# Attention pass of a graph network: seven tiles' sums ahead of the wait for the next batch, and one signal for seven tiles

## What is computed

```python
h = (x @ W_gat).reshape(n, H, C)
a_s = jnp.sum(h * att_src, axis=-1)
a_d = jnp.sum(h * att_dst, axis=-1)
e = a_s[src] + a_d[dst]
e = jnp.where(e >= 0, e, NEG_SLOPE * e)
m = jax.ops.segment_max(e, dst, num_segments=n)
alpha = jnp.exp(e - m[dst])
den = jax.ops.segment_sum(alpha, dst, num_segments=n)
alpha = alpha / den[dst]
msg = h[src] * alpha[..., None]
agg = jax.ops.segment_sum(msg, dst, num_segments=n)
```

## Time and profile before

| | us |
|---|---|
| median of 3 runs | 6590.89 |
| lowest and highest | 6564.43, 6594.76 |
| the profiled execution | 6602.38 |
| its span | 6600.6 |
| in it, from the first gather of the attention pass to its end | 2194.8 to about 3600 |

### The profile page before, as it was taken

The page is one execution under the profiler, slowest core; times in us unless marked ns, Lnnn a source line. Parts: engine busy times, 40 slices in busy tenths (PEclk is TensorE's granted clock), DMA queues, the critical chain, the costliest instruction groups (busy, mean ns, idle before and its releaser), DMA issues.

```text
span 6600.6 us, 99072 instructions
## 1 busy us (share of the span) xinstructions
PE 4910.2 (74%) x36573; PEld 4058.1 (61%) x36573; DVE 2714.1 (41%) x7772; ACT 1025.3 (16%) x2929; POOL 1522.1 (23%) x1600
## 2 busy tenths in 40 slices
PE   2888378787776244444445549999999999999998
PEld 2555255555554234434434238888888888888887
DVE  5888444454444445444446452222222222222222
ACT  3888311111112000000000320000000000000000
POOL 1000155565552455555553000000000000000000
PEclk8999688888887566666666779999999999999999
DMA  3111211111110222222221024444444444444444
GB/s 115 75 74 75 61 51 53 50 53 49 49 50 23 72 68 72 71 64 64 70 72 46 0 74 150 146 146 151 146 151 146 146 151 146 151 146 146 151 146 146
DMA packets 235594, 629.91 MB, mean 95 GB/s; under 512 B 64193, under 2 KB 129639, under 8 KB 235104
## 3 DMA queue, kind: packets, MB, share of 16 engines
q1 hardware_dynamic: 184688, 520.10, 24.0%
q0 software_dynamic: 50688, 107.11, 6.1%
HBM read 568.80 MB, written 58.59 MB: 95 GB/s over the span
## 4 chain that ended last, share of the span: by engine, by line
PE 64%; DVE 12%; issue 10%; another core or an unknown queue 10%; ACT 3%; SPq 1%; DMA 1%; POOL 0%; DVEq 0%; ACTq 0%; POOLq 0%
PE ps L1384 23%; PE pt L1384 17%; PE ps L1221 11%; PE pt L1421 4%; PE ps L1410 3%; PE ps L1272 2%; DVE E L1742 2%; ACT A L855 1%; PE pt L1205 1%; DVE B L1797 1%; DVE arena L1838 1%; ACT E L1057 1%; DVE C L1528 1%; PE ps L1353 1%
## 5 line engine op out<-in xcount | busy, mean ns | idle before, releaser
L1221 PE MATMUL ps<-E,arena 128*128 128x288 f32 (+7 forms) x3116 | 876.7, 437 | 316.2 <-DVE E L1742 238.7
L723 POOL DMA_INDIRECT arena<-table,src_i x782 | 743.1, 950 | 1209.0 <-DMA table<-A 667.6
L738 POOL DMA_INDIRECT E<-gat_table,src_i x782 | 754.1, 964 | 739.9 <-DVE arena L1838 382.5
L1221 PEld LDWEIGHTS ps<-E,arena 128*128 128x128 f32 x3116 | 551.8, 210 | 580.0 <-DVE E L1742 270.1
L1384 PE MATMUL ps<-E,arena 128*128 128x256 f16 x6860 | 762.0, 274 | 108.5 <-DVEq L1994 97.3
L1384 PEld LDWEIGHTS ps<-E,arena 128*128 128x128 fp8e4 x6860 | 674.6, 98 | 190.9 <-issue 109.7
L1384 PE MATMUL ps<-A,arena 128*128 128x256 f16 x6860 | 762.1, 274 | 14.0 <-DVE A L2017 14.0
L1384 PEld LDWEIGHTS ps<-A,arena 128*128 128x128 fp8e4 x6860 | 674.8, 98 | 96.4 <-issue 15.2
L1742 DVE SCALAR_TENSOR_TENSOR E<-arena,pt 128x512 f32<-128x512 bf16 x782 | 553.4, 744 | 318.0 <-PE ps L1221 223.1
L1272 PE MATMUL ps<-arena,B 128*128 128x144 f32 x2332 | 537.5, 384 | 60.9 <-issue 58.6
L1384 PE MATMUL pt<-E,arena 128*128 128x256 f16 x5145 | 567.4, 273 | 0.0
(11 more groups left out here) (305 smaller groups left out, 4115.8 us busy)
## 6 DMA issues: line engine op xcount, KB each, us to landing
arena<-adj SPq DMA_DIRECT2D x497, 784.0 KB, 4.3
adj<-E SPq DMA_DIRECT2D x49, 784.0 KB, 3.3
O<-dst_rows SPq DMA_DIRECT2D x112, 224.0 KB
arena<-table,src_i POOLq DMA_INDIRECT x782
E<-gat_table,src_i POOLq DMA_INDIRECT x782
E<-in_etype SPq DMA_DIRECT2D x781, 16.0 KB
weight_e<-tile_flags SPq DMA_DIRECT2D x216, 32.0 KB
rel_i<-tile_flags SPq DMA_DIRECT2D x216, 32.0 KB
```

Source lines behind the costliest of these rows:

```text
L723: pool.indirect_dma_start(out=rows_ring[:, k % RING, :], out_offset=None, in_=table, in_offset=bass.IndirectOffsetOnAxis(ap=src_i[:, k:k + ...
L738: pool.indirect_dma_start(out=att_rows[:, b % 3 * AB + at, :], out_offset=None, in_=gat_table, in_offset=bass.IndirectOffsetOnAxis(ap=src_ ...
L1221: mm = pe.matmul(ps[m % 4][:, (lo - WD * m) * BASES:(hi - WD * m) * BASES], rows_ring[:, k % RING, :], m_ring[:, k % MS, lo - first_dst(k) ...
```

## The change

In PE's round the sums of tiles 0 to 6 of batch b-1 come first, ahead of the wait for `staged` and of the turn of batch b. Then k runs from 0 to 6 alone: two expansions of batch b and the sum of tile 7 + k of batch b-1. The carrying products and the transposes stay after k = 2 and k = 5. `aggregated` is raised once for each half of seven tiles (and at the last tile), and the values that ACT and DVE wait for are counted in halves.

```diff
@@ ACT @@
-                            act.wait_ge(sem("aggregated"), near_last[i] + 1)
+                            act.wait_ge(sem("aggregated"), near_last[i] // AH + 1)
...
-                            act.wait_ge(sem("aggregated"), AB * (b - 1))
+                            act.wait_ge(sem("aggregated"), 2 * (b - 1))
@@ PE @@
-                    mm.then_inc(sem("aggregated"), 1)
+                    if k % AH == AH - 1 or tile == TILES - 1:
+                        mm.then_inc(sem("aggregated"), 1)
 
                 for b in range(ABATCHES + 1):
+                    if b >= 1:
+                        for k in range(AH):
+                            aggregate(b - 1, k)
                     if b < ABATCHES:
                         pe.wait_ge(sem("staged"), b + 1)
                         if b:
                             pe.wait_ge(sem("joined"), b)
                         pe.transpose(heads_turned, stage[:, b % 2, :, :].rearrange("p h t -> p (h t)"), ident[:, :]
                                      ).then_inc(sem("turned"), 1)
-                    for k in range(AB):
-                        if b < ABATCHES and k < AH:
+                    for k in range(AH):
+                        if b < ABATCHES:
                             expand(b, 2 * k)
                             expand(b, 2 * k + 1)
                         if b >= 1:
-                            aggregate(b - 1, k)
+                            aggregate(b - 1, AH + k)
@@ DVE @@
-                        dve.wait_ge(sem("aggregated"), min(AH * (g - 2), TILES))
+                        dve.wait_ge(sem("aggregated"), g - 2)
...
-                        dve.wait_ge(sem("aggregated"), AB * (b - 1))
+                        dve.wait_ge(sem("aggregated"), 2 * (b - 1))
```

## The result

The changed kernel takes 6625.25 us (median of 20 runs, 6586.99 to 6658.07), the kernel before, run beside it, 6584.44 us (20 runs, 6541.41 to 6620.12). The ratio is 1.0069, with a 95% interval of 1.005 to 1.0089: **slower by 0.7%**, some 41 us. The forecast was +89 us. The direction and most of the picture in the trace were right; the size was about twice what came.

What follows compares the result with a forecast made beforehand. It took PE's signals, late while POOL gathers, as the bound; 74 us over 49 batches plus 15 us at the end made +89 us, 6691 us profiled, 6680 us as median; range 6380 to 6850 us.

Steps and rivals of the forecast that it cites:

- The bound: Attention pass: no engine full; PE's signals reach waiters late while POOL gathers, stopping POOL about 7.5 us a batch.
- step 3: PE: seven sums of 6.5 us put the turn 6.3 us after POOL's restart R, the scan 4.7 us later.
- The edge at R+8: PE's signals: prompt until about 8 us after POOL's restart R, late behind that.
- Step 4: Carry, transposes and last expansions move into the late stretch: 26.5 us a batch for 24.98, together +89 us.
- the pattern's 25.3: Batch from 2305.78: POOL's gathers 17.5 us, late signal 2.4, DVE and ACT until restart 5.3.
- rival C: No change: every batch exactly like the one from 2305.78, +30 us, 6621 us; chance 0.13.
- rival B: Worse: the carry late in each batch, all at 29.9 us, +256 us, 6847 us; chance 0.17.
- Step 1: Fourteen `aggregated` signals a batch become two on PE: nothing gained or lost.
- Steps 2 and 5: Removing the products at a batch's end on PE, and ACT's stage with SP's flag transfers: nothing from either.
- Rival D: Faster: lateness comes from the number of PE's signals; 18.5 us a batch, -303 us, 6288 us; chance 0.14.
- Rival E: Faster by less: signals clear soon, sums take 3.0 us; 21.9 us a batch, -151 us, 6440 us; chance 0.16.
- The listed signs: Trace after: turn at R+6 to R+7, gathers in fourteens, stops of 7 to 12 us, scan idle 4 us.

Runs made afterwards that it cites:

- ahead14: Changed kernel with all 14 sums of the batch before ahead of the turn, not seven; one run, 6750.42 us.
- order_only: Changed kernel with the sums of tiles 0 to 6 still ahead of the turn, but `aggregated` signalled at each tile as before; ratio 1.0068 to the kernel before.
- sparse: Changed kernel without most sums of tiles 7 to 13 of each batch (part of the aggregation left out); 24.09 us a batch.

## Why the prediction was right or wrong

**The bound and step 3.** Right in kind. PE's signals, late while POOL gathers, were what held both kernels; the sums went ahead of the turn, the turn from R-2 behind R. The edge at R+8 was not right: carries that left between R+5.2 and R+8.4 were taken 1.3 to 12.1 us late in the changed kernel. Nor do signals clear only when POOL has stopped: the expansions that ended at 2560.93 were taken at 2566.01, R+13.7 of a run whose gathers went on until 2569.88. Wrong in size: R+6.3 was taken, R+4.6 is the mean. The seven sums took 3.8 us in the batch shown, not 6.5 (18 records, where 20.8 were taken): I had set all of them at the slower level of the clock. Windows of 2 us in that batch, in the columns of the earlier trace rows, show the granted clock rise while they run and just behind them, from 0.50, which is 1.2 GHz, to 1.00, which is 2.4, after 14.3 us in which PE had stood idle:

```profile
3010.00:3012.00 2.00, 2.00 (x9) 2.00 (x10) 2.00 (x5) 0.00 (x0) 1.70 (x2) 0.50 0.17 35
3012.00:3014.00 2.00, 2.00 (x17) 1.99 (x16) 0.20 (x2) 0.17 (x1) 1.39 (x3) 0.77 0.56 137
3014.00:3016.00 2.00, 2.00 (x22) 1.94 (x22) 0.84 (x2) 0.12 (x1) 1.70 (x2) 1.00 0.71 197
```

**Step 4, the term that failed.** The period: 26.5 us taken, 25.49 measured. I had added 1.2 us to the pattern's 25.3 because the carry's signal would leave at R+9 and be caught in some batches. It left at R+5 to R+8.4, since the turn was earlier. DVE's L1817 did take it late in every batch, at R+7.2 to R+17.9 and once at R+20.0, but that cost something only in 5 of 52, where the second reduction came behind R+20.3; in the worst, from 3492.67, the batch took 28.7 us. **So the step that failed is the price of a caught carry:** 1.2 us a batch was put on it, and it cost 0.2 at most, because the last expansions were caught until R+20 all the same and hid it. With the 25.3 of the pattern that stood in the same paragraph the sum would have been 0.3 x 49 + 15 = +30 us; that is rival C, to which I had given 0.13. The truth lies between, nearer to C. In numbers: 49 x 0.50 = 24.8 us in place of 74, 2.4 us for the first batches in place of 0, and 10.5 us at the end in place of 15 (from batch 54's first gather to the last turn 66.2 us, where it had been 55.8): 37.6 in place of 89 us. ahead14 measures the mechanism behind the term that I had feared: with the turn and the carry caught in nearly every batch a batch costs 27.25 us, and 28.5 to 28.6 where the carry is caught until R+20, not 29.9, so rival B's price was too high as well.

**What I hadn't seen** is why the two patterns lie so near each other. The late stretch isn't a threshold at R+8 and a clearing "1 to 4.4 us after POOL has stopped". By the measured moments it ends at 1.42 to 1.43 us a gather: 20.0 us for 14, 39.7 for 28. That is why it was 2.4 us behind a run of 14 and 4.4 us behind one of 28; both numbers stood in the prediction. A batch costs 19.9 to 20.0 us of this in either pattern. Before, 39.7 us and 10.7 us of chain made 50.4 us for two batches; now 20.0 and 5.3 make 25.3 for each. Had I divided the two clearing times by their gathers I would have had that.

**Step 1**, nothing from fewer signals: right (1.0005, and order_only like the whole change). **Steps 2 and 5**, nothing: nothing in the traces speaks against them, and no run isolates them. **Rival D** fell with step 1; what it said of 18.5 us a batch without lateness was near to the 17.67 that the last runs showed, where POOL and not the chain set it. **Rival E** (21.9 us a batch) fell: the sums were nearly as short as it asked (3.8 us for 3.0), but the last signal still had to wait for R+20.

**The listed signs**: runs of 14, stops of 7 to 12 us (7.9 to 8.1 us in most), no run of 28, the second reduction 2.6 us behind POOL's last gather: as forecast. Not as forecast: the turn at R+6 to R+7 (it came at R+3.1 to R+6.3), and DVE's scan idle for 4 us (median 2.8).

## What to carry to other kernels

When a waiter stands still though its producer is long done, plot the moment at which it is released against the start of what else runs: if it falls on one grid whatever the producer did, the cost may be a shared service, and shifting the producer's work by a few microseconds buys or costs almost nothing. An order of instructions is worth what it moves past the wait that ends last; here both orders met the same 20.0 us a batch, and the loss of 0.5 us was only the remainder. Before tuning against such a wait, run the unchanged kernel at several times and on several chips: an edit that gained 1.6% where signals were late sets its own pace of 22.8 us a batch where 17.7 are to be had.

## What the runs showed of the hardware

- A gather of POOL has a second price beside the 1.25 us of its issue: where signals are late, 1.42 to 1.43 us, independent of its rows (64 or 128), after which PE's signals get through. Runs of 7, 12, 14 and 28 gathers hold the last of them until R+10.0, R+17.2, R+20.0 and R+39.7; single PE products start 0.7 us apart in that stretch, half of 1.43. What it is that both share was not found.
- Only PE's signals are late in that stretch: a signal of DVE to PE took 0.05 to 0.06 us in all 52 batches, and caught signals of PE are raised one behind the other, within 0.12 us in the batch shown (3029.88, 3029.94, 3030.00).
- With a break of POOL of 2.5 us after each seven gathers hardly a signal is caught; either order with these waits is 1.5 to 1.6% faster than the kernel before. An idle time of 1.36 us did not end the lateness (sparse, at 2846.48).
- Whether the lateness is there is a matter neither of the kernel nor of one chip: the kernel before took 6584 to 6632 us in the first four sets of runs and 5867 to 5869 us in the last three, and one chip showed both. What switches it is open.
- The number of PE's completion signals (7 or 19 a batch) has no effect within 0.2%.
